# Two shared parts in units among blocks 48 to 111, a third plane on TensorE, and steps reordered in rounds and middle

## The reference, cut to what matters

```python
h = _layernorm(x, axis=-1) * (1 + ca) + sa
x = x + ga * _L0_attn_ref(h, ...)
h = _layernorm(x, axis=-1) * (1 + cb) + sb
x = x + gb * _L0_ffn_ref(h, ...)
...
# attention: no softmax, so keys by values are summed once for a batch
kv = jnp.einsum('bshd,bshe->bhde', k, v)
num = jnp.einsum('bshd,bhde->bshe', q, kv) * scale + vsum[:, None, :, :]
den = jnp.einsum('bshd,bhd->bsh', q, ksum) * scale + seq_len
o = num / den[..., None] + lepe_conv(v, lepe_w, lepe_b)
...
# experts
shared_out = jax.nn.silu(x @ shared_gate_w.T) * (x @ shared_up_w.T) @ shared_down_w.T
_, top_idx = jax.lax.top_k(corrected, TOP_K)
hmid = jax.nn.silu(gate) * up
out = jnp.einsum('teh,te->th', y, combine) + shared_out
```

## Time and profile before

| | us |
|---|---|
| median of 3 runs (817.01 to 818.91) | 817.6 |
| the profiled execution, its own time | 820.11 |
| its span, first to last instruction | 818.3 |

### The profile page before, as it was taken

How to read it: one execution, slowest core, us unless ns; L and a number is a source line. 1 busy time by engine, 2 the same in 40 slices (tenths; PEclk the granted TensorE clock), 3 DMA queues, 4 the chain that set the end, 5 groups by cost and what they waited for, 6 DMA issues and landing times.

```text
span 818.3 us, 16697 instructions
## 1 busy us (share of the span) xinstructions
PE 755.9 (92%) x4282; PEld 586.7 (72%) x4283; DVE 490.1 (60%) x1323; ACT 449.8 (55%) x1168; POOL 412.2 (50%) x420
## 2 busy tenths in 40 slices
PE   4997999899999978888999999999999999999996
PEld 4665657575765745556999998888888999995554
DVE  3456578858867983273545545545444445547996
ACT  5376265576436424423777776667777777771000
POOL 0000000177757767776777777777756666662000
PEclk9996599989979999999999999999999999999999
DMA  9400001033413587765677877777777666588991
GB/s 331 143 0 1 0 1 52 8 129 128 173 65 121 212 298 289 306 221 181 205 223 250 259 256 241 247 240 225 230 225 233 185 188 194 159 315 305 412 387 52
DMA packets 82452, 157.33 MB, mean 192 GB/s; under 512 B 14410, under 2 KB 55503, under 8 KB 82256
## 3 DMA queue, kind: packets, MB, share of 16 engines
q1 hardware_dynamic: 58192, 95.68, 36.3%
q0 software_dynamic: 19968, 56.67, 18.3%
q10 hardware_dynamic: 4224, 4.19, 1.5%
HBM read 87.10 MB, written 73.56 MB: 196 GB/s over the span
## 4 chain that ended last, share of the span: by engine, by line
PE 73%; DVE 12%; DMA 5%; ACT 3%; issue 3%; SPq 2%; POOL 1%; DVEq 0%; ACTq 0%; POOLq 0%
PE ps_wide L1207 19%; PE ps_wide L1215 10%; PE ps_wide L972 7%; PE ps_wide L847 5%; PE ps_narrow L1196 5%; DMA expert_outs<-arena,dest 3%; PE ps_wide L994 3%; PE ps_wide L1138 2%; PE ps_narrow L985 2%; PE ps_kv L994 2%; PE ps_wide L965 2%; PE ps_kv L1253 2%; PE ps_narrow L1253 2%; PE ps_wide L1012 2%; DMA arena<-expert_rows 2%
## 5 line engine op out<-in xcount | busy, mean ns | idle before, releaser
L496 POOL DMA_INDIRECT expert_rows<-arena,slot_i x192 | 194.2, 1011 | 230.8 <-DVE arena L1482 164.3
L510 POOL DMA_INDIRECT expert_outs<-arena,dest x224 | 217.8, 972 | 101.8 <-issue 57.5
L1207 PE MATMUL ps_wide<-arena 128*128 128x128 f32 x1792 | 238.5, 277 | 2.3 <-ACT arena L751 2.3
L1207 PEld LDWEIGHTS ps_wide<-arena 128*128 128x128 f32 x1792 | 219.3, 193 | 2.8 <-ACT arena L751 2.6
L763 ACT COPY arena<-arena 128x512 f32 x224 | 138.4, 619 | 43.4 <-issue 14.4
L1662 DVE TENSOR_TENSOR arena<-arena,ps_wide 128x128 f32<-128x128 f32 x224 | 64.6, 288 | 162.3 <-ACT arena L757 96.4
L1215 PE MATMUL ps_wide<-arena 128*128 x448 | 135.2, 384 | 5.5 <-DVE arena L1662 5.5
L751 ACT COPY arena<-ps_narrow 128x256 f32<-128x256 f32 x224 | 83.3, 372 | 67.3 <-PE ps_narrow L1196 64.5
L1672 DVE TENSOR_SCALAR arena<-ps_wide,arena 128x256 f32<-128x256 f32 x224 | 107.6, 480 | 1.5 <-PE ps_wide L1215 0.7
L1196 PE MATMUL ps_narrow<-cst,arena 128*128 128x128 f32 x448 | 86.1, 274 | 1.9 <-DMA arena<-expert_rows 1.9
L1196 PEld LDWEIGHTS ps_narrow<-cst,arena 128*128 128x128 f32 x448 | 62.5, 141 | 25.6 <-DMA arena<-expert_rows 3.5
(11 more groups left out here) (227 smaller groups left out, 968.3 us busy)
## 6 DMA issues: line engine op xcount, KB each, us to landing
arena<-expert_rows SPq DMA_DIRECT2D x224, 160.0 KB, 2.7
arena<-expert_outs SPq DMA_DIRECT2D x48, 512.0 KB, 11.9
arena<-w_experts SPq DMA_DIRECT2D x32, 384.0 KB, 7.8
expert_rows<-pad_row SPq DMA_DIRECT2D x33, 160.0 KB, 1.8
out<-x ACTq DMA_DIRECT2D x8, 512.0 KB, 8.3
expert_outs<-arena,dest POOLq DMA_INDIRECT x224
x<-x SPq DMA_DIRECT2D x3, 1024.0 KB, 11.3
h_cols<-arena SPq DMA_DIRECT2D x6, 512.0 KB, 3.6
```

The costliest lines, as they stand in the source:

```text
L496: nc.gpsimd.indirect_dma_start(rows, bass.IndirectOffsetOnAxis(ap=slots_i[b % 2][:, t, k:k + 1], axis=0), hrows[b % 2][:, t, :], None, bou ...
L510: nc.gpsimd.indirect_dma_start(outs, bass.IndirectOffsetOnAxis(ap=dest[:, u:u + 1], axis=0), yb[:, u, :], None, bounds_check=last_out, oob ...
L1207: last = mm(ps_wide[:, 0, u % 2, half * P:(half + 1) * P], wgu[:, u % 4, first:first + I], xbt[:, u % 2, c * P:(c + 1) * P], start=(c == 0 ...
```

## The change

Six edits. (1) In the first body VectorE takes the bounds of the gates and the gated projection ahead of the second pair of rotations, two taps and the mask ahead of the inverse roots. (2) In every round TensorE takes the fourth numerator behind the turned denominators, and the last turned rows and the next batch's first turn ahead of the first spreading. (3) In the middle SiLU 0 stands between the sums and the squares, SiLU 1 behind the scaling; VectorE adds part 1 ahead of the ranks and multiplies part 2 ahead of the slots; TensorE takes gate 3 ahead of down 2 and turns the first block ahead of down 3; ScalarE copies the first block ahead of the weights. (4) Parts 6 and 7 (`AMONG`) leave the tail. They are done in four units of two tiles each, one in each of the steps 3 to 6 (blocks 48 to 111), in `ps_kv` and in a place of their own. Their columns are loaded with those of parts 0 and 1. (5) SP waits for the four units before it loads the columns of parts 4 and 5, which lie where the units' place was; only these two are loaded after block 119. (6) In the tail TensorE sums three planes of the parts at places 3, 5 and 7, and VectorE adds three; each `add_planes` now stands right ahead of its `close`.

```diff
@@
-BY_DVE, BY_PE = [0, 1, 2, 3], [4, 5]
+BY_PE = [[3, 4, 5] if n in (3, 5, 7) else [4, 5] for n in range(8)]
+BY_DVE = [[k for k in range(TOPK) if k not in by_pe] for by_pe in BY_PE]
...
-LAST = list(range(BEFORE, PARTS))
-TAIL = [0, 1, LAST[0], 2, LAST[1], 3, LAST[2], LAST[3]]
+LAST, AMONG = [BEFORE, BEFORE + 1], [BEFORE + 2, BEFORE + 3]
+TAIL = [0, 1, LAST[0], 2, LAST[1], 3] + AMONG
+UNIT = PART // 2
+UNITS = [(i, n) for i in AMONG for n in range(PART // UNIT)]
...
+FIRST_UNIT = FULL // UNROLL - len(UNITS)
@@ SP
+            for i in AMONG:
+                load_h2(i)
...
+                if g == HALFWAY + 1:
+                    sp.wait_ge(s_ud, len(UNITS))
@@ ScalarE
+                if norm and b == B - 1:
+                    shared_silu(0)
                 act.wait_ge(s_means[norm], b + 1)
...
-                if not front:
-                    shared_silu(0)
-                    shared_silu(1)
...
                     second_norm(a)
                     if front:
                         copy_v(1)
+                    else:
+                        shared_silu(1)
...
+            act.wait_ge(s_slot, B + 1)
+            copy_block(0, 0, True)
             act.wait_ge(s_wall, 16 * E)
             act.wait_ge(s_sd, BEFORE)
-
-            act.wait_ge(s_slot, B + 1)
             for j in range(3):
                 copy_weights(j, j, True)
-            copy_block(0, 0, True)
@@ TensorE, rounds
-                        if t % 2 == 0:
+                        if t in (0, 2, 4):
                             numerator(t // TPH, t // 2 % C)
...
-                    if first:
+                    numerator(1, 1)
+                    if back:
+                        turn_rows(3)
+                    if follows:
                         turn_next(0)
                     pe.wait_ge(s_rdx, b + 1)
                     broadcast(0)
-                    if back:
-                        turn_rows(3)
-                        if follows:
-                            turn_next(0)
                     pe.wait_ge(s_numc, b * HALVES + 1)
@@ TensorE, blocks
+            def unit_gate_up(n):
+
+                i, at = UNITS[n]
+                if at == 0:
+                    pe.wait_ge(s_h2p[i], 16)
+                if n:
+                    pe.wait_ge(s_ux, n)
+                else:
+                    pe.wait_ge(s_table, 3)
+                for a, w in enumerate((wsg, wsu)):
+                    for m in range(C):
+                        for c in range(C):
+                            last = mm(ps_kv[:, a, m * UNIT * P:(m + 1) * UNIT * P], w[:, c, m * P:(m + 1) * P],
+                                      shared_cols[i][c][:, at * UNIT * P:(at + 1) * UNIT * P], start=(c == 0), stop=(c == C - 1))
+                last.then_inc(s_ug, 1)
+
+            def unit_down(n):
+
+                pe.wait_ge(s_um, n + 1)
+                for t in range(UNIT):
+                    for c in range(C):
+                        last = mm(ps_kv[:, 0, t * D:(t + 1) * D], unit_mid[:, c, t * P:(t + 1) * P], wsd[:, c, :],
+                                  start=(c == 0), stop=(c == C - 1))
+                last.then_inc(s_ud, 1)
...
+                    if u == 4 and with_unit:
+                        unit_gate_up(g - FIRST_UNIT)
+                    if u == 8 and with_unit:
+                        unit_down(g - FIRST_UNIT)
+
+            shared_gate(3)
+            shared_down(2)
+            shared_up(3)
+            turn_block(0, 0, 0, True, False)
+            shared_down(3)
+            pe.wait_ge(s_wall, 16 * E)
@@ VectorE
+                    dve.wait_ge(s_qk, 2)
+                    bound_gates(0)
+                    gate_projection()
                     rotate(1, 1, 3)
                     rotate(1, 0, 4)
-                    dve.wait_ge(s_qk, 4)
-                    bound_gates(0)
-                    gate_projection()
                     sum_v()
-                    convolve(range(1, 2))
+                    convolve(range(1, 3))
+                    mask_kv()
                     dve.wait_ge(s_squares[0], 2)
                     inverse_roots(0, 1)
                     second_columns()
-                    convolve(range(2, 3))
-                    mask_kv()
...
                     choose()
+                    shared_add(1)
                     take_ranks()
+                    shared_mid(2)
                     slots()
...
+            def unit_multiply(n):
+
+                dve.wait_ge(s_us, n + 1)
+                v.tensor_tensor(unit_mid, unit_mid, ps_kv[:, 1].rearrange("p (c n) -> p c n", c=C), ALU.mult).then_inc(s_um, 1)
...
             add_planes(2)
             shared_mid(LAST[1])
-            add_planes(3)
             close(2)
-            close(3)
...
+            for n in range(3, PARTS):
+                add_planes(n)
+                close(n)
```

95 lines of the change are left out of this document (42 added, 53 removed).

## The result

| | before | after |
|---|---|---|
| median, measured side by side (9 runs each) | 818.01 us | 814.13 us |
| ratio, 95% interval | | 0.9955, 0.9939 to 0.9971 |
| the profiled execution, its own time | 820.11 us | 816.07 us |
| its span | 818.3 us | 814.2 us |

The account below looks back on a forecast made before the run. TensorE was taken as the bound only among the blocks and in the tail, elsewhere waiting for others. Terms -12.4 - 6.2 + 14.9 - 0.5 - 7.6 = -11.8 took 817.6 to 805.8 us, range 799.5 to 812.0.

Parts of the forecast that it names:

- The rounds: Four rounds up to the middle: 12.4 us sooner, from 9.0 in the first, 2.9 and 0.5 in the others.
- the fourth numerator's new place: Rounds 2 to 4: behind the turned denominators, so VectorE's run of slots comes 0.96 us sooner in each.
- The middle: Rounds' end to first block's gate: copies of the columns 2.7 us sooner, first gate 6.7 sooner, 6.2 at block 48.
- the rule against the change: TensorE's clock: throttled by default, released by activity; a shorter round or the middle's new 3.4 us gap may throttle again.
- First gate to block 48: Early blocks: GpSimd's pace lets only 6.2 of the middle's 6.7 us reach block 48.
- 112 to 160: Blocks with 3.3 us of waits while SP issues column loads; two of four loads move: 0.5 us sooner.
- The units: Blocks 48 to 111: four units cost 20.7 us less 7.3 idle time; with 0.4 and 1.1 added, 14.9 later.
- the 1.1 for refills: Blocks 48 to 111: allowance in us for refilling the pipeline at all eight insertions of units.
- Rivals 3 and 4: Units among the blocks: 3, each insertion refills the pipeline, 823.2 (0.06 at 812 to 823); 4, units hidden, GpSimd paces (given nothing).
- The tail: Last stage: VectorE is late next, 30 operations from its third close, ending 807.3 instead of 814.9: 7.6 us sooner.
- Rival 2: Tail turns to DMA: loads 3 us later make the last product wait, 807 to 809; chance 0.04.
- rival 1: Half rate moves: against, first round and middle's logits, 811.1 (0.05 above 811); for, 794.3 (0.12 below 800).

Follow-up runs that it names:

- e4_silu_alone: The kernel before with only the two SiLUs of the middle moved as in the change: 818.42 us (10 runs), ratio 0.9997.
- the tail's edit: Changed kernel with up 1 whole in the middle's gap, plus part 3's planes added ahead of VectorE's third close: tail 67.1 or 67.2 us, 68.1 to 68.2 without.

## Why the prediction was right in six stages and wrong in one

**The rounds** (forecast 12.4, measured 13.6). The first round is right in mechanism: the mask starts as the sums end, the numerators run at the full rate, the half rate stays in part of the round. It gave 10.3 for 9.0. The other three gave 0.3, 1.7 and 1.3, together 3.3 for 3.4, and this agreement is in good part luck. I had 0.96 in each for the fourth numerator's new place. VectorE's work on the turned denominators does come 0.9 sooner in the third round, but 0.5 in the fourth and not at all in the second, where the clock is at 0.55 and 0.60 from 142 to 146 (1.00 before). The end of the third round's slow spreading, for which I had 0.5, gave 1.4; the three first output projections together, by their rates, gave 0.5 (6.4, 5.4 and 5.4 for 16 records; before 6.7, 4.7 and 6.2).

**The middle** (forecast 6.7 sooner, measured 2.3 later). This is the step that failed. I wrote that the copies of the columns start 2.7 sooner: they start 3.2 sooner, relative to the gate. I wrote "the new 3.4 us gap in the middle, where TensorE waits for the column copies, may too" under the rule against the change: the gap came, of 3.12 us. I worked out the half rate only for the logits' own 6.3 us of work, at most 3.4, and left it out of the sum. Measured: 23 us at half rate and 9.1 lost, 6.0 of them in the logits alone. What was wrong in it is the length: I took it for granted that the clock would be back after one stretch of steady work. The trace of the kernel before has a case against that, in the very round of the earlier trace rows, of which I showed two microseconds: behind the 5.00 of idling TensorE was busy without a stop from 70 to 82, and the clock stayed at 0.50, as it did until past 98:

```profile
70.00:82.00 12.00, 12.00 (x32) 7.93 (x33) 4.76 (x4) 9.77 (x39) 0.00 (x0) 0.50 0.00 0
```

With the clock held the middle is 60.2 to 60.3, where the forecast had 59.7. The Trainium skill (TensorE: Matmul & The Clock Gate, Part 1) has the throttled state as the default and activity as what releases it; the trace agrees for the fall, at 3.12 us of waiting here. For the return it shows a busy TensorE at 0.50 for 23 us in one execution and, in e4_silu_alone's, a clock that is back in under 4.

**First gate to block 48** (+0.5, +0.4) and **112 to 160** (-0.5, -0.3). Right in number. GpSimd now starts its output scatterings at 379.56, 7.9 sooner; VectorE's waits for a landed scattering, 19.9 us before, are down to 6.5. The first forecast was made for a gate that comes 6.7 sooner; in the two kernels where the middle did shorten by 6 us, the stretch takes 78.3 and 79.1, beside 78.4 before.

**The units** (14.9, 15.0). Right in the total, with two errors that cancel. The idle time there was 5.1 us and not 7.3, and the units cost 20.1 in all, so the 1.1 for refills did not show: TensorE has no idle time over a microsecond at any unit. (The pace in the forecast, 97.3 / 63, is 1.544 and not 1.546; that is 0.1 us over 64 blocks.) Rivals 3 and 4 are dead.

**The tail** (7.6, 8.0). Right in the operation count (VectorE: 37 us from its third close on), in the wait (5.2 for 5.11) and in what the DMA engines do to VectorE, which never waits for planes. Rival 2 is dead. TensorE, though, waits 1.74 us for planes near 796 and is done at 801.5, not by 796 as I had it; VectorE asks for that last sum at 807.12.

So rival 1, against me, was the case that came, in the middle, and its price was not 3.4 but 9.1. The range's upper end took in 3.4 of it, at 811.1.

## What to carry to other kernels

A step that shortens a chain on one engine can open a gap on TensorE where there was none. Price the half rate behind a gap over all the work that follows until a row shows the clock back, not over the next operation alone; the kernel before had such a row, 12 us long. Put that price into the sum if the gap is as long as one at which the trace has the clock fall. It is a price with a chance, since a gap of the same length brought it in one round and not in another. The remedy is cheap: fill the gap with work that is due anyway (up 1 as a whole, instead of among the logits), and only if there is none, with redundant matmuls, in a gap that is at the full rate when it begins. And when one wait in a pipeline goes, write down what the very next operation needs, too: the tail's edit gave 1.0 for 2.5 because I stopped one step early and counted an operation too many.
